# Grouped attention layers: 24 batches written one behind the other instead of a loop over pairs, and one order of work for all four tiles

## The reference

```python
xn = rmsnorm(x, norm_w)
q = (xn @ wq).reshape(B, T, N_HEADS, HEAD_DIM)             # 16 heads of 32 columns
k = (cond @ wk).reshape(B, S, N_KV_HEADS, HEAD_DIM)        # 4 key/value heads
v = (cond @ wv).reshape(B, S, N_KV_HEADS, HEAD_DIM)
qg = q.reshape(B, T, N_KV_HEADS, n_rep, HEAD_DIM)          # 4 query heads to a key head
scores = jnp.einsum('btgrd,bsgd->bgrts', qg, k) * scale
attn = jax.nn.softmax(scores.astype(jnp.float32), axis=-1)
out = jnp.einsum('bgrts,bsgd->btgrd', attn, v).reshape(B, T, N_HEADS * HEAD_DIM)
return residual + out @ wo
```

## Time and profile before

| | us |
|---|---|
| median of 3 runs | 4277.11 |
| the profiled execution | 4275.98 |
| its span, first to last instruction | 4274.2 |
| of it, `grouped_layers`, from 2138 us on | 2136.2 |
| PE busy in the span | 4082.7 (96%) |
| DVE busy | 2467.5 (58%) |
| ACT busy | 2075.9 (49%) |
| POOL busy | 1999.9 (47%) |

### The profile page before, as it was taken

The page is one execution under the profiler, slowest core; times in us unless marked ns, Lnnn a source line. Parts: engine busy times, 40 slices in busy tenths (PEclk is TensorE's granted clock), DMA queues, the critical chain, the costliest instruction groups (busy, mean ns, idle before and its releaser), DMA issues. The chain is left out here.

```text
span 4274.2 us, 62243 instructions
## 1 busy us (share of the span) xinstructions
PE 4082.7 (96%) x19496; PEld 2641.2 (62%) x19496; DVE 2467.5 (58%) x3453; ACT 2075.9 (49%) x2648; POOL 1999.9 (47%) x1072
## 2 busy tenths in 40 slices
PE   9999999997999999999969999999999999999999
PEld 7888888885556665565544555555555555555555
DVE  3122300014565556555667777777777787777775
ACT  3111211123354344444437666666666676666665
POOL 0000000003465556555526666666566666666666
PEclk9999999998999999999979999999999999999999
DMA  5333522225454445445433323333333333333332
GB/s 182 129 135 135 170 82 84 83 96 135 118 135 128 120 122 138 122 121 132 125 91 83 85 81 96 85 93 92 91 86 82 84 106 91 86 80 82 95 80 64
DMA packets 316053, 451.85 MB, mean 106 GB/s; under 512 B 45176, under 2 KB 117368, under 8 KB 315832
## 3 DMA queue, kind: packets, MB, share of 16 engines
q1 hardware_dynamic: 315832, 448.86, 37.3%
HBM read 217.72 MB, written 102.77 MB: 75 GB/s over the span
## 5 line engine op out<-in xcount | busy, mean ns | idle before, releaser
L1895 DVE TENSOR_REDUCE a_max_cols<-a_ps 128x1 f32<-128x512 f32 x1536 | 1015.7, 672 | 342.4 <-PE a_ps L2038 339.1
L1780 ACT ACTIVATE a_probs<-a_ps 128x1024 f32<-128x1024 f32 x768 | 785.0, 1025 | 645.5 <-PE a_ps L2069 640.2
L2038 PE MATMUL a_ps<-a_k_ops,a_q_ops 96*128 96x512 f32 x1536 | 660.2, 441 | 62.0 <-DVE a_max_cols L1895 46.5
L1689 POOL TENSOR_TENSOR a_sums<-a_probs 128x1024 f32<-128x1024 f32 x192 | 455.9, 2390 | 328.7 <-ACT a_probs L1780 327.5
L2038 PEld LDWEIGHTS a_ps<-a_k_ops,a_q_ops 96*128 96x128 f32 x1536 | 292.9, 191 | 437.6 <-DVE a_max_cols L1895 240.9
L1036 DVE TENSOR_REDUCE a_max_cols<-a_ps 128x1 f32<-128x512 f32 x522 | 346.0, 686 | 350.7 <-PE a_ps L1189 350.7
L2069 PE MATMUL a_ps<-a_q_ops,a_k_ops 128*128 128x512 f32 x1536 | 496.8, 405 | 1.5 <-ACT a_q_ops L1771 0.9
L803 POOL MEMSET a_ident<- 128x128 f32 x1 | 0.2, 207 | 975.6 <-issue 975.6
L1689 POOL TENSOR_TENSOR a_sums<-a_sums,a_probs 128x1024 f32<-128x1024 f32 x192 | 453.8, 2386 | 0.1
L2083 PE MATMUL a_ps<-a_probs,a_v 128*32 128x512 f32 x3072 | 412.8, 610 | 7.8 <-issue 6.9
L303 DVE TENSOR_TENSOR cp_c_lo<-cp_raw,cp_c_hi 128x1024 fp32r<-128x1024 f32 x64 | 78.4, 1225 | 529.4 <-ACT cp_c_hi L247 529.4
(11 more groups left out here) (131 smaller groups left out, 7330.2 us busy)
## 6 DMA issues: line engine op xcount, KB each, us to landing
a_k_ops<-k_scratch SPq DMA_DIRECT2D x201, 256.0 KB, 3.9
a_q_ops<-a_qn_hi SPq DMA_DIRECT2D x768, 64.0 KB, 2.0
k_scratch<-cp_out SPq DMA_DIRECT2D x88, 512.0 KB, 2.8
a_q_ops<-a_qn_hi SPq DMA_DIRECT2D x268, 128.0 KB, 2.3
cp_raw<-in_ctx_t SPq DMA_DIRECT2D x64, 512.0 KB, 4.1
x_raw<-out_t SPq DMA_DIRECT2D x25, 1024.0 KB, 7.0
a_q_ops<-a_qn_lo SPq DMA_DIRECT2D x384, 64.0 KB, 2.0
a_x_res<-out_t SPq DMA_DIRECT2D x92, 256.0 KB, 2.9
```

Of the source, the lines that this page charges most:

```text
L1689: pool.tensor_tensor(sums[:, hp], (probs if n < H else sums)[:, hp], probs[:, n], ALU.add)\
L1780: act.activation(probs[:, n], ps[:, 2 * (n % 2):2 * (n % 2) + 2, :], ACT.Exp).then_inc(exped, 1)
L1895: dve.tensor_reduce(max_cols[:, t % 2, col:col + 1], bank(b), AX.X, ALU.max, negate=True)\
L2038: pe.matmul(bank(b), q_ops[0:SHIFT, s, h, q * P:(q + 1) * P], k_ops[0:SHIFT, s, :], start=True, stop=True).then_inc(smax, 1)
```

## The change

The loop, the cut into two parts and the second order of slot 3 go. Every batch number is a Python number, so every semaphore is waited for at a constant, and `where` decides while the program is built and leaves no branch in it. The instructions that compute are the same, in the same numbers, on every engine.

```diff
         def pairs(engine, batch):
-            for it in range(2):
-                batch(it, it)
-            with engine.Fori(1, N // 2 - 1) as j:
-                batch(2 * j, 0)
-                batch(2 * j + 1, 1)
-            for it in range(2):
-                batch(N - 2 + it, it)
+            for it in range(N):
+                batch(it, it % 2)
...
         @block.tensor
-            def first_part(it, t, par):
-
-                scores(it, t, 0)
...
-                scores(it, t, 4)
-                maximum(it, t, 8)
-                if t < T - 1:
...
+            def batch(it, par):
+                for t in range(T):
+                    scores(it, t, 0)
...
+                    outputs(it, t, 0, par)
...
+                    if t == T - 1 and there(it, 2 * T):
+                        pe.wait_ge(q_taken, tile_no(it, t) + AHEAD + 1)
+                        sum_squares(it + 2, FB)
+                    maximum(it, t, 7)
+                    scores(it, t, 4)
+                    maximum(it, t, 8)
                     project_out(it, t, par, 0)
                     maximum(it, t, 9)
                     project_out(it, t, par, 1)
...
                     maximum(it, t, 10)
                     project_out(it, t, par, 2)
                     project_out(it, t, par, 3)
-                else:
-                    maximum(it, t, 9)
-                    scores(it, t, 5)
-                    maximum(it, t, 10)
-                    for tile in range(T):
-                        project_out(it, t, par, tile)
-
-            def second_part(it, t, par):
-                if t == T - 1:
-                    outputs(it, t, 1, par)
-                    maximum(it, t, 11)
-                else:
                     maximum(it, t, 11)
                     outputs(it, t, 1, par)
-                turn(*at(it, t + 1))
-                scores(it, t, 6)
...
-            def batch(it, par):
-                for t in range(T):
-                    if there(it, t - 1):
-                        second_part(*at(it, t - 1), par if t > 0 else 1 - par)
-                    first_part(it, t, par)
+                    turn(*at(it, t + 1))
+                    scores(it, t, 6)
...
             pairs(pe, batch)
-            second_part(N - 1, T - 1, 1)
             outputs(N - 1, T - 1, KT - 1, 1)
```

More of the change, by code:

```diff
@@ L1824, in second_part @@
-            def second_part(it, t, par):
[L1825 to L1833, removed]
             def batch(it, par):
                 for t in range(T):
+                    exponential(it, t, 0)
@@ new lines, in batch @@
+                    exponential(it, t, 1)
+                    if isinstance(it, int) and it == 0 and t == 0:
+                        squares(1)
+                    if t == 1 and there(it, T):
+                        act.wait_ge(q_taken, (it + 1) * T)
+                        inv_rms(it + 1)
+                    exponential(it, t, 2)
+                    exponential(it, t, 3)
+                    if there(it, t + AHEAD):
+                        round_q(*at(it, t + AHEAD))
+                    exponential(it, t, 4)
@@ new lines, in batch @@
+                    if t == 0 and there(it, T):
+                        round_x(it + 1, 0)
+                    if t == 2 and there(it, 2 * T):
+                        squares(it + 2)
+                    exponential(it, t, 5)
+                    if t == 0 and there(it, T):
+                        round_x(it + 1, 1)
+                        where(act, it, par, B - 1, lambda: round_wq(it // B + 1))
+                    exponential(it, t, 6)
+                    if there(it, t + 1):
+                        shift(*at(it, t + 1), 0)
@@ L1841, in _ @@
+                    exponential(it, t, 7)
+                    if there(it, t + 1):
+                        shift(*at(it, t + 1), 1)
             squares(0)
@@ new lines, in batch @@
+            def batch(it, par):
+                for t in range(T):
+                    scores(it, t, 0)
+                    maximum(it, t, 0)
+                    outputs(*at(it, t - 1), KT - 1, par if t > 0 else 1 - par)
+                    denominators(*at(it, t - 1))
+                    maximum(it, t, 1)
+                    scores(it, t, 1)
+                    maximum(it, t, 2)
+                    project_q(*at(it, t + AHEAD), range(1))
+                    maximum(it, t, 3)
+                    project_q(*at(it, t + AHEAD), range(1, 2))
+                    scores(it, t, 2)
+                    maximum(it, t, 4)
+                    project_q(*at(it, t + AHEAD), range(2, 3))
+                    maximum(it, t, 5)
+                    project_q(*at(it, t + AHEAD), range(3, 4))
+                    scores(it, t, 3)
+                    maximum(it, t, 6)
+                    outputs(it, t, 0, par)
+                    if isinstance(it, int) and it == 0 and t == 0:
+                        pe.wait_ge(q_taken, AHEAD + 1)
+                        sum_squares(1, FB)
+                    if t == T - 1 and there(it, 2 * T):
+                        pe.wait_ge(q_taken, tile_no(it, t) + AHEAD + 1)
+                        sum_squares(it + 2, FB)
+                    maximum(it, t, 7)
+                    scores(it, t, 4)
+                    maximum(it, t, 8)
```

155 lines of the change are left out of this document (59 added, 96 removed).

## The result

The changed kernel takes 4227.42 us (median of 4 runs, 4227.01 to 4228.98), where the kernel before took 4278.84 beside it (4 runs, 4276.88 to 4283.81): 0.9879 of the time, interval 0.9862 to 0.9896. Forecast were 4226, range 4218 to 4245. The span of the profiled execution fell from 4274.2 to 4227.0 us, by 47.2; the medians differ by 51.4.

The account below looks back on a forecast made before the run. PE, busy 96% of the span, was taken to bound the kernel. From 4275.98 us, 30.8 for the jumps and 19.0 for the order came off, 0 for register steps and weight work, giving 4226.2; range 4218 to 4245.

Parts of the forecast that it names:

- The jumps: PE's nine jumps back, in slot 3: windows of 87.73 us become 84.31, 30.8 us off, bounds 20 to 31.
- Register steps and `If`s: On every engine in each looped batch: hidden behind PE's matmuls, 0 us, between 0 and 1 for all 20 batches.
- The order: One order in slot 3 removes two waits of `maximum` for DVE: 0.87 us a batch, 19.0 in all, bounds 0 to 22.0.
- the tight place: Slot 3, `project_out` part 0 due just after `mean_square` ends: up to 0.1 us of wait, against 0.44 before.
- Weight work: `rest_wo` in batches 1, 9, 17: PE's stop stays; taken as 0, between 4.2 us gained and 1.4 lost by the clock.
- A: Slot 3: waits for `mean_square` or reductions replace those removed, only the jumps count; 4245.2 us; chance 12%.
- B: The pause belongs to work every second batch, not the jump; only the order counts, 4257 us; chance 3%.
- C: Slower: straight code must be loaded while it runs; 4306 us at two stops a batch; chance 4%.

Follow-up runs that it names:

- e1: The kernel before, with its old cut and old order of slot 3, but all 24 batches written out on every engine; 4244.07 us, 0.9922 of before.
- e3: The kernel before, old order, with PE's batches alone written out and the other engines still in the loop; 4244.92 us, 0.9926 of before.
- e5: The changed kernel with nine short jumps back added on PE where the long ones had been; 4230.33 us, 0.9873 of before.
- f1: The kernel before with 128 instructions that do nothing ahead of PE's stage, moving its later code; 4261.86 us, 0.9960 of before.
- e7: The changed kernel with `outputs` 1 ahead of `maximum` 11 on PE in the five slots without `project_out`; 4230.15 us, 0.9876 of before.
- e2: The kernel before with its loop and cut, but PE has the new order in slot 3 too; 4269.99 us, 0.9985 of before.
- e6: The kernel before with four batches in a turn of the loop, 4 jumps back instead of 9; 4260.35 us, 0.9952 of before.
- e4: The kernel before, old order, with PE in the loop and the four other engines written out; 4276.83 us, 1.0002 of before.
- e8: The changed kernel with the four vector instructions of `rest_wo` spread behind `maximum` 3 to 6; 4233.75 us, 0.9884 of before.

## Why the prediction was right

*The jumps*: forecast 30.8 us. e1 gives 31.2 in the windows, e3 31.2 with PE alone. The mechanism was named rightly: e5 rules out the branch instruction, f1 shows that the place of the code counts, and the packets show the two blocks that each jump brings. What the prediction didn't see is how much of the 3.42 us is chance: 2.56 of it hang on where the target lies, with the falls of the clock behind it.

*Register steps and `If`s*: forecast 0 to 1 us; 0.05 us a batch in e1, 1 us for 20.

*The order*: forecast 0.87 us a batch, measured 0.79, and slot 3 ends at 21.43 and not at 21.28. `project_out` waits for `mean_square` by the 0.1 us that stood there as the bound of the tight place. For batch 0 the sign was wrong: forecast a gain of 0.2, measured 20.23 against 19.37 us. Its slot 3 has no `project_out`, so `maximum` 11 comes right behind `maximum` 10 and waits for DVE; e7, with the old order there, takes 19.38. The prediction had said that this slot has less work and not asked what then stands between the maxima. What the order is worth also depends on the loop, as e2 shows; in the changed kernel, where both are done, the sum held because the order's price had been taken from windows without a jump.

*Weight work*: forecast 0, between a gain of 4.2 and a loss of 1.4. Batches 9 and 17 together gained 2.7 beyond the order's 0.79 each, as their clock fell less (1.00 and 0.98 where it was 0.98 and 0.96). The window of batch 1 lost 2.5: 0.9 is the slot 3 of batch 0 just told, the rest the clock, at 0.98 behind the same waits. That need not be the change's doing: in e6, whose batches 0 and 1 are written as in the kernel before, this window takes 88.79 us at 0.94. The stop itself stayed at 2.6 us, as forecast.

*Rivals*: A (the waits move) happens in batch 0 and, with 0.10 us, at `mean_square`. B (not the jump) is out by e3 and e4. C (straight code has to be loaded) is out: a straight batch brings 3 or 4 packets on the queue in question, a looped one without a jump 4, and PE has no wait named issue left in batches 2 to 21.

*What was luck.* The span fell by 47.2 us, and 49.8 were forecast. The order gave about 16.4 us (15.8 in batches 2 to 21, a loss of 0.9 in batch 0, and the 1.5 behind batch 21, if all of that is the order's) and not 19.0, and the clock gave back 2.7 in batches 9 and 17, where nothing was forecast. The jumps were right on their own; that the other two nearly cancel was not foreseen.

## What to carry to other kernels

A jump back cost time here on PE, which bounds the kernel, and on no other engine: write out PE's side first, or shift the loop's code and look whether the second stop goes, before giving up loops on the others. Price a jump by the windows that hold one against those that don't, not by the stops that the waits name, since the clock that falls behind them is part of the price. Before moving an instruction of DVE that reads two operands from SBUF, look what POOL does at that moment.

## What the runs showed of the hardware

- One and the same jump costs PE 3.42 us, or 0.86 when its code lies 128 instructions further on; a jump to a near target costs nothing (83.54 against 83.52 us a batch).
- Each jump back of PE brought two extra packets of 256 instructions (98 packets for 20424 instructions, where straight code has 70 for 17900). The second stop went, and the packets did not, when the code was shifted by 128 instructions.
- Written-out code streamed through batches 2 to 21 without a stop of PE named issue, with fewer packets than the loop.
- A vector instruction of two SBUF operands took 2.74 us in place of 0.68 when it started 0.17 us behind POOL's sum, in all three batches of e8 alike (PE's waits for it sum to 6.6 us in 3). It ended 0.55 us after POOL's instruction each time, and POOL's next one, which started meanwhile, took 2.80 to 2.83 us, where 2.39 is the mean in the changed kernel. `x_lo` of the changed kernel, with two SBUF operands too, takes 0.67 to 0.68 us where it starts beside no instruction of POOL, and up to 2.01 where it does. The Trainium skill, page "SBUF — State Buffer", section "SBUF: two separate sides", says that the two engines share a pair of ports which one of them holds for a whole instruction; the trace agrees.
- The clock fell behind a stop of 2.6 us in some of the windows and not in others: batch 9 of the changed kernel 1.00, batch 17 0.98 after the same stop. What decides it stays open.
